# Four chained attention layers: normalisation moved to ScalarE, low halves to GpSimd, weight folds spread out

## The reference

```python
x = L0(x)   # batchnorm; depthwise 3x3 conv + 1x1 to q, k, v; k and v resized to 7x7; softmax attention (4 heads,
            # relative bias); depthwise 3x3 conv + 1x1; + x; then batchnorm, relu, 1x1 (mlp), + residual
x = L1(x)   # group norm (8 groups); k softmax over channels, q softmax over points; context = k^T v; q context; 1x1; + xn
x = L2(x)   # group norm (32 groups); full attention over 196 points, 8 heads; 1x1; + x
x = L3(x)   # group norm (32 groups); full attention, one head of 256 channels; 1x1; + x
```

## Time and profile before

| | us |
|---|---|
| median of 3 runs | 2170.71 (2168.53 to 2171.08) |
| the profiled execution: time | 2170.37 |
| the profiled execution: span from first to last instruction | 2168.3 |
| busy: TensorE, VectorE, ScalarE, GpSimd | 2076.3, 1820.4, 1527.8, 1278.3 |
| mean granted TensorE clock, as a share of the full 2.4 GHz | 0.976 |

### The profile page before, as it was taken

How to read it: one execution, slowest core, us unless ns; L and a number is a source line. 1 busy time by engine, 2 the same in 40 slices (tenths; PEclk the granted TensorE clock), 3 DMA queues, 4 the chain that set the end, 5 groups by cost and what they waited for, 6 DMA issues and landing times.

```text
span 2168.3 us, 58678 instructions
## 1 busy us (share of the span) xinstructions
PE 2076.3 (96%) x15232; PEld 1686.7 (78%) x15232; DVE 1820.4 (84%) x4359; ACT 1527.8 (70%) x5172; POOL 1278.3 (59%) x2954
## 2 busy tenths in 40 slices
PE   4679999999999999999999999999999999999987
PEld 3466888888888788888878888887888888788775
DVE  6778899988888998988899898888989888887532
ACT  2256777777777777777777777777777777777763
POOL 2455666666666666666666666666666666664311
PEclk8799999999999999999999999999999999999977
DMA  3000011001101100110110011011101100100000
GB/s 126 15 23 23 16 39 39 29 23 37 37 22 37 37 30 22 37 37 22 37 37 30 22 37 37 23 36 37 37 15 37 37 31 28 38 31 24 24 23 23
DMA packets 29828, 70.22 MB, mean 32 GB/s; under 512 B 6261, under 2 KB 7105, under 8 KB 29761
## 3 DMA queue, kind: packets, MB, share of 16 engines
q1 hardware_dynamic: 26928, 67.68, 9.0%
q10 hardware_dynamic: 2832, 1.73, 0.3%
HBM read 30.86 MB, written 12.85 MB: 20 GB/s over the span
## 4 chain that ended last, share of the span: by engine, by line
PE 91%; DVE 3%; POOL 2%; issue 2%; ACT 1%; SPq 1%; DMA 0%; POOLq 0%; DVEq 0%; ACTq 0%
PE ps_c L1166 19%; PE ps_a L1166 17%; PE ps_e L1166 17%; PE ps_b L1166 17%; PE ps_s L1166 10%; PE ps_s L1216 8%; POOL gn_t L579 1%; PE ps_a L1292 1%; DVE y L1158 1%; PE ps_e L1454 0%; PE ps_e L1292 0%; PE ps_b L1454 0%; PE ps_e L1399 0%; SPq L475 0%; ACT e L827 0%
## 5 line engine op out<-in xcount | busy, mean ns | idle before, releaser
L827 ACT ACTIVATE e<-ps_s,nm 98x196 f32<-98x196 f32 x1024 | 426.1, 446 | 89.9 <-DVE nm L956 89.8
L590 POOL TENSOR_SCALAR xn<-x,gn_scale,gn_shift 128x196 f32<-128x196 f32 x384 | 353.2, 933 | 20.8 <-POOL gn_shift L585 20.8
L1158 DVE SCALAR_TENSOR_TENSOR y<-opad,w_dw,y 128x406 f32<-128x406 f32 x512 | 301.8, 645 | 0.0
L1139 DVE SCALAR_TENSOR_TENSOR y<-xpad,w_dw,y 128x406 f32<-128x406 f32 x512 | 300.8, 640 | 0.0
L956 DVE TENSOR_REDUCE nm<-ps_s 98x4 f32<-98x784 f32 x256 | 240.6, 962 | 41.8 <-PE ps_s L1166 41.8
L834 ACT COPY pt<-ps_s 98x392 f32<-98x392 f32 x512 | 229.1, 503 | 42.6 <-PE ps_s L1216 41.8
L568 POOL TENSOR_TENSOR gn_t<-gn_group 128x4 f32<-128x4 f32 x96 | 34.3, 358 | 372.9 <-DVE gn_group L1006 286.5
L827 ACT ACTIVATION_READ_ACCUMULATOR e<-ps_s,nm 98x1 f32 x1024 | 231.6, 226 | 0.0
L1216 PE MATMUL ps_s<-w_eye,e 98*98 98x98 f32 x2048 | 204.6, 251 | 0.6 <-ACT e L827 0.6
L1216 PEld LDWEIGHTS ps_s<-w_eye,e 98*98 98x98 f32 x2048 | 186.3, 131 | 24.1 <-issue 16.2
L581 POOL TENSOR_SCALAR gn_t<-gn_t 128x4 f32<-128x4 f32 x288 | 119.7, 416 | 58.6 <-POOL gn_t L579 58.6
(11 more groups left out here) (245 smaller groups left out, 5596.8 us busy)
## 6 DMA issues: line engine op xcount, KB each, us to landing
x_in<-in_x SPq DMA_DIRECT2D x32, 392.0 KB, 3.1
x_res<-in_x SPq DMA_DIRECT2D x32, 392.0 KB, 3.3
x2b<-x SPq DMA_DIRECT2D x32, 392.0 KB, 2.6
out<-x SPq DMA_DIRECT2D x32, 392.0 KB, 2.6
out_pairs<-out SPq DMA_DIRECT2D x32, 392.0 KB, 3.5
w_q<-in_q SPq DMA_DIRECT2D x3, 256.0 KB
w_k<-in_k SPq DMA_DIRECT2D x3, 256.0 KB
w_v<-in_v SPq DMA_DIRECT2D x3, 256.0 KB
```

Source lines behind the costliest of these rows:

```text
L590: g.tensor_scalar(dst[:, c, of_image(i)], src[:, c, of_image(i)], t.scale[:, j:j + 1], t.shift[:, j:j + 1], ALU.mult, ALU.add).then_inc(t. ...
L827: s.activation(e2[:, j, tc], tile(use)[0:HALF, of_image(tc)], ACT.Exp, bias=nm2[:, j, tc:tc + 1], accum_out=den2[:, 2 * i + tc, h:h + 1]). ...
L1139: v.scalar_tensor_tensor(out=dst, in0=window(xpad, c, k, CR), scalar=tap, in1=dst, op0=ALU.mult, op1=ALU.add).then_inc(conv1_steps.sem, 1)
L1158: v.scalar_tensor_tensor(out=dst, in0=window(opad, c, k, CR), scalar=tap, in1=dst, op0=ALU.mult, op1=ALU.add).then_inc(conv2_steps.sem, 1)
```

## The change

- `normalized` on GpSimd becomes `coefficients`: the same small steps, whose last one now counts too. The twelve normalisations of a pair go to ScalarE as steps `norm1_0` to `norm3_1`, each two activations of 128x196 with scale and bias from tiles. They take over the waits on readers of the normalised tensor.
- The low halves go from VectorE to GpSimd (`low1_0` to `low3_1` in `POOL_AT`).
- The folds are cut in three: `fold_values` after the first pair's later q0 product, `fold_queries` after its scores, `fold_outputs` after its later o0. `split_weights` becomes `split_loaded` (at the old places, plain weights alone) and `split_folded`: on ScalarE after the first pair's later o0 copy, on VectorE before its first pw step. ScalarE's first relu waits for all of it; the heads get a semaphore of their own.
- All five tables and the banks are new. The first steps of TensorE move from slot 64 to 112 and its last from 714 to 755.

```diff
 PE_AT = {
-    "q0_1": 64, "q0_0": 72, "k0": 95, "s0_0": 100, "s0_1": 102, "v0": 122, "t0_1": 133, "t0_0": 134, "o0_1": 159,
-    "o0_0": 162, "pw0": 214, "pw1": 219, "mlp0": 238, "mlp1": 240, "gn1": 257, "kv0": 297, "kv1": 300, "kv2": 302,
-    "kv3": 304, "q1_0": 316, "q1_1": 321, "ctx0": 325, "ctx1": 326, "out0": 332, "out1": 333, "gn2": 344, "hk0": 382,
...
+    "q0_0": 112, "q0_1": 126, "k0": 134, "s0_0": 150, "s0_1": 152, "v0": 178, "t0_0": 181, "o0_0": 205, "t0_1": 207,
+    "o0_1": 212, "pw0": 266, "pw1": 275, "mlp0": 290, "mlp1": 292, "gn1": 304, "kv0": 344, "kv1": 347, "kv2": 358,
+    "kv3": 359, "q1_0": 361, "q1_1": 373, "ctx0": 375, "ctx1": 377, "out1": 384, "out0": 385, "gn2": 396, "hk0": 428,
...
 POOL_AT = {
-    "resize0": 0, "resize1": 16, "probs0": 64, "probs1": 96, "gn1": 240, "gn2": 304, "gn3": 544, "rows3": 592,
+    "resize0": 146, "resize1": 155, "probs0": 219, "probs1": 246, "gn1": 365, "low1_0": 384, "low1_1": 393,
+    "gn2": 448, "low2_0": 457, "low2_1": 466, "gn3": 676, "low3_0": 685, "low3_1": 694, "rows3": 740,
 }
...
-            def normalized(p, n, src, dst):
+            def coefficients(p, n):
...
-                link(g.tensor_tensor(t.shift[:], bias[:], t.t[:], ALU.subtract))
-                for c in range(KC):
-                    for i in range(2):
-                        j = 2 * c + i
-                        alone()
-                        g.tensor_scalar(dst[:, c, of_image(i)], src[:, c, of_image(i)], t.scale[:, j:j + 1],
-                                        t.shift[:, j:j + 1], ALU.mult, ALU.add).then_inc(t.done.sem, 1)
+                g.tensor_tensor(t.shift[:], bias[:], t.t[:], ALU.subtract).then_inc(t.steps.sem, 1)
...
+                    for n, src, dst, _ in splits:
+                        for c in range(KC):
+                            p = pair_of(t, u, POOL_AT[f"low{n}_{c}"])
+                            if p is not None:
+
+                                pool.wait_ge(gn[n].high.sem, gn[n].high.at(p, c + 1))
+                                g.tensor_tensor(dst[:, 1, c], src[:, c], dst[:, 0, c], ALU.subtract).then_inc(gn[n].low.sem, 1)
...
+            def split_loaded():
+
                 act.wait_ge(weights_in, WEIGHTS)
...
+                for high, low, src in early_sources()[:PLAIN]:
                     s.copy(high, src).then_inc(early_high, 1)
...
+            def split_folded():
+
+                act.wait_ge(fold_filled, FOLDS)
+                for high, low, src in early_sources()[PLAIN:]:
+                    s.copy(high, src).then_inc(early_high, 1)
+                s.copy(heads[:], w["heads"][:]).then_inc(heads_set, 1)
...
+                    for n, src, dst in ((1, x1, xn1), (2, x2, xn2), (3, x3, xn3)):
+                        for c in range(KC):
+                            p = pair_of(t, u, ACT_AT[f"norm{n}_{c}"])
+                            if p is not None:
+                                act.wait_ge(gn[n].steps.sem, gn[n].steps.at(p + 1, 0))
...
+                                for i in range(2):
+                                    j = 2 * c + i
+                                    s.activation(dst[:, c, of_image(i)], src[:, c, of_image(i)], ACT.Identity,
+                                                 scale=gn[n].scale[:, j:j + 1], bias=gn[n].shift[:, j:j + 1]
+                                                 ).then_inc(gn[n].done.sem, 1)
...
+                            if is_first(p) and use == latest("q0_0", "q0_1"):
+                                fold_values()
...
+                            if is_first(p) and use == latest("s0_0", "s0_1"):
+                                fold_queries()
...
+                            if is_first(p) and use == latest("o0_0", "o0_1"):
+                                fold_outputs()
```

114 lines of the change are left out of this document (60 added, 54 removed), and 59 rows, old and new, of tables (ACT_AT, BANK_USES, DVE_AT, PE_AT).

## The result

The changed kernel takes 2179.74 us (median of 6 runs, 2177.56 to 2181.06) against 2170.76 us of the kernel before on the same chip (6 runs, 2168.53 to 2171.08). The ratio is 1.0044, with a 95% interval of 1.0033 to 1.0055: 9 us slower. The forecast was 2165, faster. The profiled execution has a span of 2178.7 us, 10.4 more than before.

The account below looks back on a forecast made before the run. TensorE, busy 63.03 of 63.10 us a steady round, was taken as the bound. Start -4.5, normalisations +3.5, queue +1.5, VectorE -2.5 and GpSimd stalls -3.5 gave -5.5 us: 2165 us, range over all 2154 to 2180.

Parts of the forecast that it names:

- The order on TensorE changes no instruction, so its 63.03 us stand: Steady part: TensorE's reordering was taken to leave each round at 63.03 us, a term of 0.
- Rival 2: Steady rounds: TensorE waits in every one, 0.5 us a pair, giving 2181 us; chance 0.16.
- The loop of layer two: Steady part, group product to hk0: chain of 13.2 us under 13.7 us of products, 0.5 us to spare, cost 0.
- Start, -4.5: First pair: splitting the folds starts the softmax and second convolution earlier; -4.5 us (-6 to -2) after payback.
- The payback: Start: output folds between first pair's o0 and second pair's q0 delay later steps; 0.5 us shows.
- the cover: Start: VectorE's 3.13 us of idling before pw0, expected to hide nearly all its 3.5 us of added low halves and steps.
- Normalisation path, +0.7 each: Filling and end: first normalisation to product takes 4.0 us instead of 3.27, +0.7 a traversal, +3.5 us in all.
- Stalls of GpSimd, -3.5: Filling: two coefficient steps held by VectorE's tap bursts (6.24, 5.22 us) get shorter; -3.5 us (0 to -11).
- rival 3: Filling: low halves on GpSimd caught behind bursts, 3 traversals of 3 to 5 us, 2174 to 2180; chance 0.08.
- Queue behind the normalisation: Filling, ScalarE: copies queue behind the wait for layer one's coefficients, delaying the second convolution; +1.5 us (0 to +3.6).
- VectorE's relief: Filling: VectorE loses 3.5 us a pair of low halves and no longer queues behind high halves; -2.5 us.
- Life of a pair, 0: Draining: a pair's life on TensorE goes from 650 to 643 slots, but the last pair's dependences are unchanged; 0.

Follow-up runs that it names:

- a12_fullrows: Changed kernel, order untouched, with the two 8-row products made 128 rows deep by zero rows: 2167.52 us, ratio 0.9988 to the kernel before.
- b1_apart: Kernel before with one exchange on TensorE, hq1 placed between the two 8-row products rep0 and rep1: 2189.23 us, ratio 1.0095.
- b5_fullrows: Kernel before with only the two 8-row products made 128 rows deep by zero rows: round 62.73 us against 63.06.
- a2_cutlow: Changed kernel with low halves of all pairs but the first cut to 8 of 392 columns: 2177.73 us, ratio 1.0035.
- b3_oldtable: Changed kernel's code with the timetable and bank table of the kernel before: 2305.16 us, ratio 1.0620.
- a11_poolnorm: Changed kernel and timetable, but normalisations back on GpSimd, low halves staying there: 2203.50 us, ratio 1.0153.
- a4_foldstart: Changed kernel with all folds of weights back in front of the first product: 2180.10 us, ratio 1.0064.
- b6_folds: Kernel before with the change's split folds alone, in its own timetable: 2.6 us less time (0.4 to 4.6).
- b7_folds_full: Kernel before with both the split folds and the 8-row products at full depth: 17 us below the kernel before.
- a10_join: Changed kernel with 8-row products beside scores, t0_1 earlier, and av0 to av2 in other banks, meant directly behind the next scores: 2202.50 us, ratio 1.0150.

## Why the prediction was wrong, point by point

- **"The order on TensorE changes no instruction, so its 63.03 us stand"**: this step failed, and it decides. The round is 63.63 us, not 63.03, with the same instructions. TensorE's time is not the sum of its instructions. A border between products of different depth or width costs 60 to 260 ns, one behind a group product 104 to 434, and the new order has worse ones, 0.54 us a round by the table. a12_fullrows (order kept, shape changed, -0.51 us a round), b1_apart (order changed alone, +0.63, of which 0.39 at borders) and b5_fullrows (-0.33) show from three sides that borders cost this much. Of the 0.57 us, 0.17 is shown by runs to be the 8-row products'; for the other 0.40 no run stands, only the table. The Trainium skill (TensorEngine Tiling (Array Packing), Key Properties) states that changing the tiling mode, as opposed to the tile, drains TensorE. The traces agree in part: the borders of products of 8 or 32 rows and of av, 32 columns wide, cost. Two things don't follow from the rule: the product rt, 8 columns wide, costs 6 ns going in and 30 coming out before, and the group products, of full depth and width, cost 104 ns and more. The page gives no figure; here it is 60 to 260 ns for the former. The prediction didn't weigh this rule, and it spoke against the change.
- **Rival 2** had the right place (the steady round), sign and size (0.5 us a pair, 2181), by a wrong mechanism: a wait for a low half. a2_cutlow puts that wait at 0.02 us a round. The time, 2179.74, lies at the very edge of the range over all, 2154 to 2180, on the side that had a chance of 0.24; that it lies inside is luck, since no term of the forecast stood for the borders. The sign named for rival 2, a round over 63.13 us, is what showed it; "no idle time on TensorE" was of no use, since the loss between products counts as busy.
- **The loop of layer two**: 13.7 us of products and 13.2 of chain were forecast. It is 14.4 and 14.4, without room: coefficients took 9.4 us where 8.5 were taken, normalisation, high and low 4.2 where 3.85 were. It costs nothing even so: a2_cutlow, with room in the loop, gains 0.02 us. b3_oldtable waits here in each round, a11_poolnorm does not.
- **Start, -4.5**: q0 23.59 (23.1), softmax 39.02 (37.9), conv2_0 51.6 (50.2), so -3.9 there. The payback was taken as 0.5 and is 3.7 in the profiled execution: the folds took 10.9 us and not 6.4 to 9, all at the lower clock, and the cover of 3.13 us on VectorE was gone, for which the text had named 3.5. In the six other kernels with these folds it is 0.4 to 1.3 us (what conv2_0 gains less what pw0 gains), so the 0.5 was near and the 3.7 an accident of the clock. By a4_foldstart nothing of the start's gain is left at the end; in the old timetable (b6_folds) 2.6 us are. The text's own sum for the start of the scores is 36.8, not 36.9.
- **Normalisation path, +0.7 each**: at the end of the last pair the first normalisation is at 2152.03 and the product at 2156.25, 4.2 us (4.0 forecast, 3.27 in the earlier trace rows). The activation took 0.50 us as taken, the low half 1.03 at the median and not 0.85. The row of 0.416 us did not bear out the price by which the text put the activation at 0.44: by those prices (Trainium skill, ScalarE: Activation LUTs, What ACT_TABLE_LOAD costs) an activation of 196 columns with one pointer operand is 0.35 us, an estimate.
- **Stalls of GpSimd, -3.5**: the longest coefficient steps in the same stretch are 2.9 and 3.0 us, where they were 6.24 and 5.22: 5.5 us less by this sum. Low halves were not caught behind bursts for long (1.45 us at most): rival 3 falls.
- **Queue behind the normalisation, VectorE's relief**: not tested one by one. All of filling, from the first to the fourth conv2_0, is 5.1 us longer, where the forecast had 0.5 for the payback and -1.7 for these terms, the stalls and four of the five normalisations together. The measured figure is not good enough to divide: the clock was 0.85 in this stretch and 0.89 before, and six kernels with the same first rounds have it between 151.9 and 160.0 us, against 159.1 here. Whether these terms were right stays open.
- **Life of a pair, 0**: from conv2_0 to the last output there are 568 slots before and 549 after; 568 x 63.06 / 128 = 279.8 and 549 x 63.63 / 128 = 272.9 us. A pair in the steady part thus leaves earlier; I had counted from q0 (650 and 643) and set the gain to 0. That this is why the last pair takes 6.5 us less is not shown: b6_folds, with the old slots, takes 187.3 us for the same stretch, where it was 193.2 before and is 186.7 now, at granted clocks of 0.91, 0.87 and 0.94. The clock at the end accounts for much of it.
- Why pair 3 doesn't keep what pair 0 gains stays open, and so does what the 0.40 us a round beside the 8-row products would be if gn2 could be moved without a wait.

## What to carry to other kernels

Where one engine is full, measure its rounds by the distance of one step between two pairs, not by its busy share, and treat its order as work: on TensorE, put products of small depth or width side by side, or fill them up with zero rows to the depth of their neighbours, which here gave 12 us for one edit. The two edits on the way, 8-row products at full depth and the split folds in the old timetable (b7_folds_full), gave 17 us without moving any work to another engine. A move of work to other engines that needs a new order must be charged with what that order costs. And where a tight timetable is reordered by hand, expect the next dependence to wait for a good part of what is gained.

## What the runs showed of the hardware that was not expected

- A product of 2 x 392 columns through 8 rows costs 0.17 to 0.31 us more than the same through 128 rows of which 120 are zero, by its borders alone (0.31 and 0.20 in a12_fullrows, 0.34 for two side by side in b5_fullrows).
- A product of 8 columns in front of 32-row scores costs 434 ns (114 to 120 of them are the scores' own way in), in front of a full-depth product 146 to 168, in front of transposes 104 to 106.
- Scores of 32 rows directly in front of av, 32 columns wide, cost 0.20 us less than the two apart (a10_join).
- GpSimd's subtraction of 128x392 with fp32r output took 1.03 us at the median, where 98x392 with fp32 output took 0.85.
- At the half clock, folds of one or two columns took 0.80 to 0.99 us for four instructions: the nine groups of them took 7.2 us, the two groups of 256 columns 3.6.
- The granted clock over the same output folds was 0.50, 0.73 or 1.00 from one kernel's execution to the next, and their time 10.9, 7.4 or 5.5 us.
